# Selective scan on one core: one input-term piece as a diagonal matmul, PSUM reads moved to VectorE, softplus in 1024-wide steps

## The reference

```
x_dbl = einsum('bkdl,kcd->bkcl', xs, x_proj_w)            # dts (8), Bs (16), Cs (16) per token
dts   = einsum('bkrl,kdr->bkdl', dts, dt_w)
delta = softplus(dts + dt_bias)                           # 256 channels per token
step: h = exp(delta * A) * h + (delta * x) * B            # 16 states per channel
      y = sum over the 16 states of h * C
ys = ys + Ds * xs
```

## Time and profile before

| what | value |
|---|---|
| median of 3 runs | 29705.68 us (29699.24 to 29705.95) |
| the profiled execution's own time | 29696.74 us |
| its span | 29695.1 us |
| PE busy | 24898.3 us (84%) |
| DVE busy | 25338.3 us (85%) |
| ACT busy | 25459.9 us (86%) |
| POOL busy | 23052.8 us (78%) |
| first and last product of the scan (L1154) start at | 5397.2 and 28650.4 us |

### The profile page before, as it was taken

The page is one execution under the profiler, slowest core; times in us unless marked ns, Lnnn a source line. Parts: engine busy times, 40 slices in busy tenths (PEclk is TensorE's granted clock), DMA queues, the critical chain, the costliest instruction groups (busy, mean ns, idle before and its releaser), DMA issues. The chain is left out here.

```text
span 29695.1 us, 503466 instructions
## 1 busy us (share of the span) xinstructions
PE 24898.3 (84%) x178572; PEld 20517.0 (69%) x178572; DVE 25338.3 (85%) x26926; ACT 25459.9 (86%) x50840; POOL 23052.8 (78%) x16524
## 2 busy tenths in 40 slices
PE   4999977888888888888888888888888888888877
PEld 2888844677777776777777677777776777777765
DVE  7666678888989898989899898989998989899975
ACT  2444434899999999999999999999999999999975
POOL 0000000799999999999999999999999999999961
PEclk7998978999999999999999999999999999999998
DMA  4101022333333333333333333333333333333333
GB/s 152 31 27 39 28 89 77 111 119 116 116 115 119 115 118 123 130 129 131 129 129 131 123 131 128 133 128 131 128 132 124 130 128 132 127 132 128 131 124 130
DMA packets 1456172, 3408.57 MB, mean 115 GB/s; under 512 B 98208, under 2 KB 1149248, under 8 KB 1173952
## 3 DMA queue, kind: packets, MB, share of 16 engines
q1 hardware_dynamic: 1453632, 3375.95, 32.0%
HBM read 2921.54 MB, written 454.03 MB: 114 GB/s over the span
## 5 line engine op out<-in xcount | busy, mean ns | idle before, releaser
L1120 DVE TENSOR_TENSOR_SCAN s_h<-s_da,s_h,s_db 128x512 f32<-128x512 f32 x16384 | 19688.8, 1261 | 1916.0 <-PE s_db L1020 1598.8
L1154 POOL TENSOR_TENSOR s_prod<-s_h,s_cb 128x1024 f32<-128x1024 f32 x8192 | 19578.1, 2390 | 170.9 <-DVE s_h L1120 91.3
L1020 PE MATMUL s_db<-eye,s_dxb 128*128 128x128 f32 x65536 | 8768.0, 277 | 3524.6 <-issue 1902.7
L1020 PEld LDWEIGHTS s_db<-eye,s_dxb 128*128 128x128 f32 x65536 | 7117.6, 141 | 5860.3 <-issue 4690.9
L1083 ACT ACTIVATE s_da<-s_delta,a_neg 128x512 f32<-128x512 f32 x16384 | 10924.7, 721 | 2.7 <-DVE s_h L1120 2.7
L1072 ACT ACTIVATE s_dxb<-s_dx,s_btok 128x256 f32<-128x256 f32 x24576 | 10708.0, 507 | 109.9 <-issue 65.8
L1033 PE MATMUL s_py<-eye,s_prod 128*128 128x128 f32 x65536 | 8498.3, 273 | 44.2 <-POOL s_prod L1154 44.2
L1033 PEld LDWEIGHTS s_py<-eye,s_prod 128*128 128x128 f32 x65536 | 7427.5, 141 | 55.5 <-POOL s_prod L1154 55.5
L1136 POOL TENSOR_SCALAR s_dxb<-s_dx,s_btok 128x256 f32<-128x256 f32 x8192 | 4073.6, 497 | 248.6 <-POOLq L56 165.1
L734 POOL COPY c_xi<-c_xi 128x1032 f32<-128x1032 f32 x8 | 8.4, 1046 | 5345.0 <-DVEq L626 5345.0
L480 DVE SCALAR_TENSOR_TENSOR a_sc<-a_scores,a_bias 128x512 f32<-128x512 f32 x1024 | 683.5, 689 | 690.3 <-PE a_scores L370 690.3
(11 more groups left out here) (136 smaller groups left out, 20448.2 us busy)
## 6 DMA issues: line engine op xcount, KB each, us to landing
s_cb<-c_rows SPq DMA_DIRECT2D x2048, 1024.0 KB, 4.7
s_xt<-xc_tok SPq DMA_DIRECT2D x1024, 256.0 KB, 5.2
y<-s_yt SPq DMA_DIRECT2D x1024, 256.0 KB
s_yb<-y SPq DMA_DIRECT2D x768, 256.0 KB, 5.2
xc_tok<-c_ot SPq DMA_DIRECT2D x32, 2048.0 KB, 7.5
o_y<-y SPq DMA_DIRECT2D x64, 1024.0 KB, 6.1
n_x<-in_x SPq DMA_DIRECT2D x64, 512.0 KB, 5.4
zn_t<-n_zt SPq DMA_DIRECT2D x32, 1024.0 KB, 7.3
```

Of the source, the lines that this page charges most:

```text
L1020: last = e.transpose(db[:, i % NDB, half, j * P:(j + 1) * P], dxb[:, i % NDXB, j, half * P:(half + 1) * P], const["eye"][:, :])
L1120: last = e.tensor_tensor_scan(h[:, n, half, flow], da[:, i % NDA, half, flow], db[:, i % NDB, half, flow], h[:, n, half, last_token:last_t ...
L1154: e.tensor_tensor(prod[:, i % NP_], h[:, n], cb[:, n, :].unsqueeze(1).to_broadcast([P, HALVES, T]), ALU.mult).then_inc(S["prod"], 1)
```

## The change

In the scan of every direction, and nowhere else:

- GpSimd no longer scales piece 3 of `dx`. It multiplies the 128x128 identity by B (one 128x128 `tensor_scalar`) and so writes diag(B) into a new tile `bdiag`. TensorE, in place of transposing that piece with the identity, multiplies the `dx` piece by `bdiag`, which transposes and scales at once: a float32 matmul with start and stop, not a transpose. Two of the eight operations of a turn are of this kind. GpSimd no longer waits for `dx`.
- Stage 1 (`xc` out of PSUM) goes from ScalarE to VectorE as one 1024-wide copy, and so does `leave` (`yt` out of PSUM). The next group's first total waits for the whole of `y` at once.
- dt bias enters in the dts matmul: `low` gets a row of ones (its copy becomes an Identity activation with the bias column `one_row`), and `dt_w` a ninth row with the bias. With that the Relu is one instruction of 1024 columns at stage 7 (it was two of 512 at stages 5 and 7), and `delta` one `tensor_tensor` max of 1024 columns (it was two `scalar_tensor_tensor` of 512).

```diff
-        dxb = m.sb(f"s{k}_dxb", [P, NDXB, SUBS, D_INNER])
+        dxb = m.sb(f"s{k}_dxb", [P, NDXB, SUBS_ACT, D_INNER])
+        bdiag = m.sb(f"s{k}_bdiag", [P, NDXB, SUBS - SUBS_ACT, P])
...
-                e.matmul(pr[:, 0, :], wts["dt_w"][:, 0:P], low[0:DT_RANK, :], start=True, stop=True).then_inc(S["dts"], 1)
+                e.matmul(pr[:, 0, :], wts["dt_w"][:, 0:P], low[0:DT_RANK + 1, :], start=True, stop=True).then_inc(S["dts"], 1)
...
+                e.activation(low[:, :], pr[0:ROWS_LOW, 0, :], ACT.Identity, bias=const["one_row"][:, 0:1]).then_inc(S["low"], 1)
+            elif stage == 7:
+                e.wait_ge(S["dts"], 2 * n)
...
+                e.activation(e1(s), pr[:, :, :], ACT.Relu, bias=wts["guard"][:, 0:1], scale=-1.0).then_inc(S["relu"], 1)
...
+        def prepare_dve(e, g, n, stage):
+            s = g % 2
             if stage == 1:
                 e.wait_ge(S["turned"], n)
                 if k == 0 and n >= 2:
                     e.wait_ge(S["skipped"], n - 1)
-                for half in range(HALVES):
-                    last = e.copy(xc[:, s, half, :], pr[:, half, :])
-                last.then_inc(S["xc"], 1)
...
+                e.tensor_copy(xc[:, s], pr[:, :, :]).then_inc(S["xc"], 1)
...
-                for half in range(HALVES):
-                    last = e.scalar_tensor_tensor(out=delta[:, s, half, :], in0=pr[:, half, :], scalar=wts["dt_b"][:, half:half + 1],
-                                                  in1=e1(s)[:, half, :], op0=ALU.add, op1=ALU.max)
-                last.then_inc(S["delta"], 1)
+                e.tensor_tensor(delta[:, s], pr[:, :, :], e1(s), ALU.max).then_inc(S["delta"], 1)
...
-                            for j in range(SUBS):
-                                last = e.transpose(db[:, i % NDB, half, j * P:(j + 1) * P],
-                                                   dxb[:, i % NDXB, j, half * P:(half + 1) * P], const["eye"][:, :])
+                            for j in range(SUBS_ACT):
+                                e.transpose(db[:, i % NDB, half, j * P:(j + 1) * P],
+                                            dxb[:, i % NDXB, j, half * P:(half + 1) * P], const["eye"][:, :])
+                            for j in range(SUBS_ACT, SUBS):
+                                last = e.matmul(db[:, i % NDB, half, j * P:(j + 1) * P], dx[:, i // D_STATE % 2, j, half * P:(half + 1) * P],
+                                                bdiag[:, i % NDXB, j - SUBS_ACT, :], start=True, stop=True)
...
+                        if n == 0 and g >= 1:
+                            e.wait_ge(S["y"], g)
...
-                            for bank in range(2):
-                                e.copy(flat(yt[:, 2 * bank:2 * bank + 2, :]), py[:, bank, :]).then_inc(S["y"], 1)
...
+                            e.tensor_copy(flat(yt[:, :, :]), flat(py[:, :, :])).then_inc(S["y"], 1)
...
-                            last = e.tensor_scalar(dxb[:, i % NDXB, j, :], dx[:, g % 2, j, :], btok[:, g % 2, j, n:n + 1], 1.0,
+                            last = e.tensor_scalar(bdiag[:, i % NDXB, j - SUBS_ACT, :], const["eye"][:, :], btok[:, g % 2, j, n:n + 1], 1.0,
                                                    ALU.mult, ALU.mult)
```

More of the change, by code:

```diff
@@ L870, in prepare_pe @@
                 last.then_inc(S["turnb"], 1)
-                e.matmul(pr[:, 0, :], wts["dt_w"][:, 0:P], low[0:DT_RANK, :], start=True, stop=True).then_inc(S["dts"], 1)
+                e.matmul(pr[:, 0, :], wts["dt_w"][:, 0:P], low[0:DT_RANK + 1, :], start=True, stop=True).then_inc(S["dts"], 1)
             elif stage == 6:
                 e.wait_ge(S["btok"], n)
-                e.matmul(pr[:, 1, :], wts["dt_w"][:, P:2 * P], low[0:DT_RANK, :], start=True, stop=True).then_inc(S["dts"], 1)
+                e.matmul(pr[:, 1, :], wts["dt_w"][:, P:2 * P], low[0:DT_RANK + 1, :], start=True, stop=True).then_inc(S["dts"], 1)
             elif stage == 11:
@@ L903, in prepare_act @@
                     e.wait_ge(S["scaled_pool"], (n - 1) * D_STATE)
-                e.activation(e1(s)[:, half, :], pr[:, half, :], ACT.Relu,
-                             bias=wts["guard_less_dt_b"][:, half:half + 1], scale=-1.0).then_inc(S["relu"], 1)
+                    e.wait_ge(S["db"], (n - 1) * 2 * D_STATE)
+                e.activation(e1(s), pr[:, :, :], ACT.Relu, bias=wts["guard"][:, 0:1], scale=-1.0).then_inc(S["relu"], 1)
             elif stage == 8:
-                e.wait_ge(S["relu"], 2 * n)
+                e.wait_ge(S["relu"], n)
                 e.activation(e1(s), e1(s), ACT.Exp, scale=-1.0, bias=wts["guard"][:, 0:1]).then_inc(S["exped"], 1)
@@ L914, in prepare_dve @@
             s = g % 2
-            if stage == 5:
+            if stage == 1:
+                e.wait_ge(S["turned"], n)
+                if k == 0 and n >= 2:
+                    e.wait_ge(S["skipped"], n - 1)
+                e.tensor_copy(xc[:, s], pr[:, :, :]).then_inc(S["xc"], 1)
+            elif stage == 5:
                 e.wait_ge(S["turnb"], n)
@@ L1085, in decay, with _ @@
                         last.then_inc(S["da"], 1)
+                    for i in range(AHEAD):
+                        scale(i)
+                        decay(i)
+                    for i in range(STEPS):
+                        g, n = divmod(i, D_STATE)
+                        if i + AHEAD < STEPS:
+                            scale(i + AHEAD)
+                            decay(i + AHEAD)
+                        if prepares(g + 1):
+                            prepare_act(e, g + 1, g + 1, n)
+                @block.vector
+                def _(e):
                     def leave(i):
@@ L1124, in _ @@
                             prepare_dve(e, g + 1, g + 1, n)
+                    for i in range(STEPS - LAG - 1, STEPS):
+                        leave(i)
                 @block.gpsimd
@@ L1385, in build @@
         wts["a_neg"] = [m.sb(f"a_neg{k}", [P, HALVES, D_STATE]) for k in range(DIRECTIONS)]
-        wts["guard_less_dt_b"] = [m.sb(f"gdt{k}", [P, HALVES]) for k in range(DIRECTIONS)]
         guard = m.sb("guard", [P, 1])
         d_sum, d_diag = m.sb("d_sum", [P, HALVES]), m.sb("d_diag", [P, HALVES, P])
-        wanted = [(const["eye"], eye), (const["mean"], mean), (const["group_of"], group_of)]
+        wanted = [(const["eye"], eye), (const["mean"], mean), (const["group_of"], group_of), (const["one_row"], one_row)]
         for name in _WEIGHTS:
@@ L1456, in constants @@
 def constants():
-    return {"eye": np.eye(P, dtype=np.float32), "mean": np.full((P, P), 1.0 / P, np.float32),
+    one_row = np.zeros((ROWS_LOW, 1), np.float32)
+    one_row[DT_RANK] = 1.0
+    return {"one_row": one_row, "eye": np.eye(P, dtype=np.float32), "mean": np.full((P, P), 1.0 / P, np.float32),
             "group_of": np.repeat(np.eye(GROUPS, dtype=np.float32), PER_GROUP, axis=0)}
@@ L1471 @@
     out = nc.dram_tensor("out", (TOKENS, C), F32, kind="ExternalOutput").ap()
-    build(nc, dram["x"], dram, out, dram["eye"], dram["mean"], dram["group_of"])
+    build(nc, dram["x"], dram, out, dram["eye"], dram["mean"], dram["group_of"], dram["one_row"])
     r = run_bass_kernel_spmd(nc, [{f"in_{n}": a for n, a in arrays.items()}], core_ids=[0])
```

45 lines of the change are left out of this document (10 added, 35 removed).

## The result

The changed kernel takes 29312.15 us (median of 4 runs, 29309.95 to 29331.22) against 29704.04 us before: 392 us less, a ratio of 0.987 with a 95% interval of 0.9855 to 0.9885. The forecast was 28,885. It is faster, clear of the noise, by less than half of the 819 us that were forecast.

What follows compares the result with a forecast made beforehand. GpSimd was taken as the bound in three of four directions. Savings of 384 groups x 1.53 and 128 x 1.83, together 822 us, off 29696.7 gave 28,875; with 9 us to the median, 28,885 was said, range 28,560 to 29,560.

Steps and rivals of the forecast that it cites:

- The scale's saving: GpSimd's scale in each scan step, cut from 256 to 128 columns: 0.133 us less a step, bounds 0.06 to 0.187.
- The wait at step 2: GpSimd waits for the scans of step 2, behind xc and yt on VectorE: 0.6 us once a group.
- the end of the last total: TensorE's last total of the old group, which yt waits for, ends at P+2.35, P being the product of step 0.
- The lead: How far VectorE's scans are ahead of GpSimd's need: 2.24 us before, 1.84 at most after, about 1.7 by step 1.
- The first direction: Its groups take 43.5 us, down from 45.33, with total, Ds term and projection ahead of turn(4) on TensorE.
- a second wait of 0.4 at step 4: In the first direction only, the scans of step 4 come another 0.4 us late for GpSimd.
- a sign of being wrong: The prediction called itself wrong if GpSimd waits for scans more than once a group.
- the period without waits: GpSimd's scan step with no idle time: 2.657 us, down from 2.79, so 42.5 us a group.
- The clock rival: TensorE, fuller in the scan, is granted a 0.85 clock: some 32,150 us in all; chance 0.03.
- ScalarE's relief: Work taken from ScalarE, 44.42 us a group down to 42.0, lets the gain on GpSimd through.
- The four copies: ScalarE's four 512-wide copies a group, of 0.586 and 0.589 us, are gone: 2.35 us in all.
- The rival in which waits between four even engines: Scans wait here and there for da or db, no engine saturated: 43.4 to 44.4 us a group, 29,040 to 29,550; chance 0.22.

Runs made afterwards that it cites:

- the two best versions: Changed kernel with last total ahead of turn(2) and Ds term at step 8, plus either every preparation stage one step later (28930.74 us) or xc on ScalarE (28930.05 us).

## Why the prediction was wrong

The direction was right, and so was the mechanism in the second to fourth direction; in the first a delay was missed. Three terms of the sum were too good, and together they account for the 427 us between 28,885 and 29,312 within 10 us.

- **The scale's saving.** This is the step that failed most. It was put at 0.133 us a step; measured are 0.103 (2.790 to 2.687 us). At 16 x 0.030 us a group and 512 groups this is 246 us. The fault is the column rate of 1.04 ns, said to lie between the product's 1.1 and the copy's 1.01. But 1.01 is what the copy allows with no fixed part at all, so it was an upper bound, and 1.04 lies above it. With the 0.19 us that the prediction takes as the fixed part, the same copy gives (1.046-0.19)/1032 = 0.83 ns and a saving of 0.106. The runs have 0.84 ns, on a fixed part of 0.23 us. The Trainium skill, "GPSIMD Engine Reference", section "Elementwise — side-by-side cycle accounting", gives 1.03 cycles an element, by the prediction's estimate 0.110 us for 128. The runs agree: 0.107 us from the scale's start to the product's.
- **The wait at step 2.** Put at 0.6 us, measured 0.8: some 100 us. The step that failed is the end of the last total, P+2.35 in the prediction and P+2.50 here. I let turn(2) start at P+0.12 as in the earlier trace rows, where it stands behind the transposes of `xt` as well; there they end just in time. Now the turn ahead of them is 0.23 us longer and the step 0.1 us shorter, and they end at P+0.36. The lead itself was near: `xc` starts at P+1.15, so scan(1) is 1.54 us ahead of the P+2.69 at which GpSimd wants it, where 1.7 was expected; in this order on TensorE that sets nothing, since `yt` waits for the total.
- **The first direction.** Put at 43.5 us, measured 44.91; 0.7 of the difference are the two points above, the rest is 0.7 us x 128 = some 90 us. I had a second wait of 0.4 at step 4; it is 0.55, and I did not follow what the delay of turn(4) and of the projection does later in the group: 0.12 at step 6 and 0.43 at step 13. So GpSimd waits four times a group here, which the prediction names as a sign of being wrong.

Right: the period without waits in its form, one step of GpSimd; `xc` and `yt` at 1.20 and 1.22 us; a turn of 1.12 us (15025.93 to 15027.03 above gives 1.10); PE at 41.27 us, under its bound of 42.2; the wait of `delta` for Ln gone; one wait a group in the second to fourth direction, at step 2. The clock rival did not come: 1.00 and 0.99 in the windows above, 0.965 over each of the four executions, 0.966 over the profiled one before. The claim that ScalarE's relief is what lets GpSimd's gain through is shown by the diagonal matmul alone, and by `yt` back on ScalarE, which brings the waits at steps 11 and 13 back.

Off, without a price of its own in the second to fourth direction: ScalarE at 42.58 us a group against 42.0. The four copies were taken off at their mean records, 2.35 us; two of them together cover 1.07 us, so they were worth 2.14 at most. That is 0.2 of the 0.6 us; the rest is open.

The rival in which waits between four even engines leave a group of 43.4 to 44.4 us, with 0.22, has the number: 43.8 us, and its range, 29,040 to 29,550, holds the result. Its mechanism, waits here and there, shows in the first direction alone. In the others there is one wait a group at the place that was forecast, and the versions with shorter groups still have one.

What was not tried: more than 3 product buffers or another split of the PSUM banks, which would let the first total of a group run later; and `yt` on ScalarE with the last total first. Of the 0.3 us left in the two best versions, that at step 3 is not explained further than its step. That at step 13, with `xc` on ScalarE, goes with ScalarE busy for 5614.56 of 5700 us of the second direction and with VectorE's waits for Ln, 117.7 us in the last three directions.

## What to carry to other kernels

When one engine sets the pace and others are within a few per cent, count what a moved instruction waits for, not only how long it runs: an instruction in program order ahead of the critical chain costs its wait too, and whatever stands in the shadow of that wait is free until the wait is removed. A change of order on a third engine can be worth more than either home for the moved work. Take a cost that rests on width from at least two widths of the same operation; taken from other operations it was off by a quarter, which here was over half of the error. And where rows give an upper bound, keep under it.

## What the runs showed of the hardware

A float32 matmul of 128x128 costs 0.235 us, a transpose of the same shape 0.109, and mixing them one in four within a turn costs nothing more: a turn went from 0.87 to 1.10 us, where six and two of them sum to 1.12. GpSimd's records are longer than what it does from start to start: the mean record of the 128-column scale is 377 ns, while the product starts 0.34 us behind it; distances between starts are the safer measure there.
